# One kernel of attention and routed experts: the last attention round kept apart from weight splitting, and the last two quartets routed and sent in one row ahead of the expert tiles

## What is computed

```
x = x + attn(layernorm(x), ctx, mask; Wq, Wk, Wv, Wo)
h = layernorm(x)
logits = h @ wg.T                      # 2048 rows x 8 experts
two best experts, weights renormalised
y_e = (silu(h @ w1_e.T) * (h @ w3_e.T)) @ w2_e.T
x = x + w_a * y_a + w_b * y_b
```

## Time and profile before

| what | us |
|---|---|
| median of three runs | 288.73 |
| profiled execution, its span | 289.2 |
| PE busy in it | 220.1 (76%) |
| DVE busy | 214.5 (74%) |
| ACT busy | 131.9 (46%) |
| POOL busy | 109.8 (38%) |

### The profile page before, as it was taken

How to read it: one execution, slowest core, us unless ns; L and a number is a source line. 1 busy time by engine, 2 the same in 40 slices (tenths; PEclk the granted TensorE clock), 3 DMA queues, 4 the chain that set the end, 5 groups by cost and what they waited for, 6 DMA issues and landing times.

```text
span 289.2 us, 5289 instructions
## 1 busy us (share of the span) xinstructions
PE 220.1 (76%) x1445; PEld 161.4 (56%) x1445; DVE 214.5 (74%) x619; ACT 131.9 (46%) x291; POOL 109.8 (38%) x120
## 2 busy tenths in 40 slices
PE   0787779998989988887667674688787789997620
PEld 0663456666757665665336542477566668886410
DVE  4779966688759867895977786568895568775596
ACT  5777127554665448342145546243334435453300
POOL 4310350121403070105486556104556565555530
PEclk9996579999999999979756799589899999999855
DMA  6954411353033302331602110421342232211807
GB/s 216 318 233 118 131 35 28 92 125 86 9 98 96 94 0 67 87 100 47 207 9 67 46 39 29 99 47 30 77 79 76 82 84 73 80 52 26 236 5 217
DMA packets 38108, 26.33 MB, mean 91 GB/s; under 512 B 4748, under 2 KB 35726, under 8 KB 37696
## 3 DMA queue, kind: packets, MB, share of 16 engines
q1 hardware_dynamic: 34848, 19.76, 25.5%
q0 software_dynamic: 2656, 5.40, 6.1%
q10 hardware_dynamic: 576, 0.83, 0.9%
HBM read 12.32 MB, written 6.31 MB: 64 GB/s over the span
## 4 chain that ended last, share of the span: by engine, by line
PE 42%; DVE 30%; issue 10%; SPq 8%; DMA 4%; ACT 2%; POOL 1%; another core or an unknown queue 1%; DVEq 0%; ACTq 0%; POOLq 0%
SPq L427 8%; PE bank L528 8%; DVE m_neg L1411 6%; PE bank L759 4%; PE bank L760 3%; PE bank L733 3%; PE bank L652 3%; DMA bd<-st 3%; PE bank L746 3%; PE bank L736 3%; PE bank L693 2%; PE bank L676 2%; PE bank L734 2%; PE bank L679 2%; PE bank L534 2%
## 5 line engine op out<-in xcount | busy, mean ns | idle before, releaser
L1411 DVE TENSOR_REDUCE m_neg<-bank 128x4 f32<-128x512 f32 x64 | 43.5, 684 | 15.4 <-PE bank L693 15.0
L1048 POOL DMA_INDIRECT ys<-big x39 | 38.1, 976 | 40.0 <-DVE big L1447 19.2
L923 ACT ACTIVATE big<-bank 128x512 f32<-128x512 f32 x64 | 37.4, 597 | 20.9 <-PE bank L679 20.0
L797 ACT ACTIVATE st<-bank 128x128 fp32r<-128x128 f32 (+1 forms) x78 | 22.6, 330 | 31.6 <-PE bank L746 16.1
L1004 POOL DMA_INDIRECT xg<-rows,rows_i x24 | 24.6, 1027 | 31.8 <-DVE rows_i L1218 11.6
L693 PE MATMUL bank<-bd,st 128*128 128x512 f32 x64 | 31.1, 509 | 4.7 <-DMA bd<-st 3.8
L676 PE MATMUL bank<-m_bd,ones_b 128*128 128x512 f32 x64 | 31.3, 489 | 2.1 <-ACT big L923 1.9
L759 PE MATMUL bank<-bd,st 128*128 x78 | 24.3, 332 | 9.8 <-DVE big L1447 6.2
L1355 DVE SCALAR_TENSOR_TENSOR st<-st_hi,cst,bank 128x512 fp32r<-128x512 f32 x32 | 23.3, 747 | 11.3 <-ACT st_hi L797 9.0
L1026 POOL TENSOR_TENSOR m_bd<-mT,cst 128x512 fp32r<-128x512 f32 x16 | 17.3, 1110 | 30.1 <-DVE mT L1334 30.0
L679 PE MATMUL bank<-bd,st 128*128 128x512 f32 x64 | 27.1, 423 | 0.0
(11 more groups left out here) (174 smaller groups left out, 514.0 us busy)
## 6 DMA issues: line engine op xcount, KB each, us to landing
bd<-st SPq DMA_DIRECT2D x126, 64.0 KB, 2.0
big<-xg SPq DMA_DIRECT2D x39, 64.5 KB
raw<-in_L_ffn_w SPq DMA_DIRECT2D x2, 1024.0 KB, 9.3
raw<-ys SPq DMA_DIRECT2D x6, 256.0 KB
x_all<-in_x SPq DMA_DIRECT2D x4, 256.0 KB, 4.5
rows<-in_mask_BxS_if POOLq DMA_DIRECT2D x4, 256.0 KB, 5.2
ctx_all<-in_L_ffn_w SPq DMA_DIRECT2D x1, 1024.0 KB
ctx_all<-in_ctx SPq DMA_DIRECT2D x3, 256.0 KB, 5.2
```

The source lines that it names most:

```text
L923: nc.scalar.activation(prob[n % 2][:, NJ * g:NJ * (g + 1), :].rearrange("p h q -> p (h q)"), s2[k % 2][:, :], ACT.Exp, scale=SCALE).then_i ...
L1048: pool.indirect_dma_start(ys, bass.IndirectOffsetOnAxis(xt[n % XR][:, D:RW].bitcast(I32), 0), y_sb[n % YR], None, bounds_check=PAIRS - 1, ...
L1411: nc.vector.tensor_reduce(m_neg[:, H * (b - 1) + NJ * g:H * (b - 1) + NJ * (g + 1)], s1[k % s1_ring(u)][:, :].rearrange("p (j q) -> p j q" ...
```

## The change

In the last round of attention the twelve weight pieces are no longer taken together by both engines tick by tick. ACT copies one of pieces 0 to 7 behind every second exponential, and pieces 8 to 11 behind the round. DVE's part of the round is written out by hand: heads, projections and statistics of each batch as it comes, with steps of quartet 2's routing, tables and splits between them. Quartet 2's fills come later on PE. Quartet 3 is normalised, routed and placed directly behind the round, and the loop over tiles begins behind that on PE and DVE. POOL sends two rows of quartet 2, takes the inverse deviations of quartet 3, sends the other six and then all of quartet 3, ahead of any result. The ranks of a quartet no longer need the running sum per batch: PE adds the earlier batches of the quartet by three more products, so `rk` waits for `sel` and for the `cum` of the quartets before, and `cum` is kept per quartet. The four pieces of w2 are split by DVE at tiles 0 and 1, and `other_tiles` comes at tiles 3 to 5 instead of 7 to 9. SP pads before it loads tile 15, and waits for quartet 3's rows only before tile 17. The w2 load stands behind the last block-diagonal copies.

```diff
--- before
+++ after
-LAST_FILLS = {2: [("x2T", 2)], 4: [("lg", 2)], 7: [("rk", 2)], 8: [("cn", 0)]}
-WEIGHT_STEPS = {0: [0, 1], 2: [2, 3], 3: [4], 4: [5], 8: [6], 9: [7], 12: [8], 14: [9], 16: [10], 17: [11]}
+LAST_FILLS = {7: [("x2T", 2)], 9: [("lg", 2)], 15: [("rk", 2)], 17: [("cn", 0)]}
+WEIGHT_STEPS = {1: [0], 3: [1], 5: [2], 7: [3], 9: [4], 11: [5], 13: [6], 15: [7]}
...
-                if u == NQ:
-                    sp.wait_ge(work_full, slot["V", NQ - 1] + 1)
-                    sp.wait_ge(ck_ready, NQ)
-                    sp.dma_start(raw[2], w2).then_inc(in_w2, 16)
...
+                if u == NQ:
+                    sp.wait_ge(work_full, slot["V", NQ - 1] + 1)
+                    sp.wait_ge(ck_ready, NQ)
+                    sp.dma_start(raw[2], w2).then_inc(in_w2, 16)
...
-            def open_phase(f):
-
-                if f:
-                    fill_pads()
+            def read_rows(f):
+
                 sp.wait_ge(tab_ready, f + 1)
...
+            def all_sent(q):
+                for k in range(2):
+                    sp.wait_ge(sent[q][k], 16 * QB)
+
+            rows = read_rows(0)
+            for q in range(NQ - 1):
+                all_sent(q)
             sp.wait_ge(o_full, 3 * QB)
             for n in range(NT):
+                if n == XR:
+                    fill_pads()
+                    rows += read_rows(1)
                 if n == NTS[0]:
-                    rows += open_phase(1)
+                    all_sent(NQ - 1)
+                    sp.wait_ge(padded, 16 * (E + 1))
...
+                    for b in range(QB - 1):
+                        nc.tensor.matmul(o[:, (b + 1) * E:QB * E], cst[:, C_ALL:C_ALL + P],
+                                         sel[:, b, :].unsqueeze(1).to_broadcast([P, QB - 1 - b, E]), start=False, stop=False)
+                    if q:
+                        pe.wait_ge(cum_ready, q)
+                    else:
+                        pe.wait_ge(setup_ready, 1)
+                    nc.tensor.matmul(o[:, 0:QB * E], cst[:, C_ALL:C_ALL + P], cum[:, q, :].unsqueeze(1).to_broadcast([P, QB, E]),
                                      start=False, stop=True).then_inc(work_full, 1)
+                    pe.wait_ge(cum_ready, NQ - 1)
+                    parts = [cum[:, NQ - 1, :]] + ([sel[:, b, :] for b in range(QB)] if q else [])
+                    for k, part in enumerate(parts):
+                        last = nc.tensor.matmul(o[:, 0:E], cst[:, C_ALL:C_ALL + P], part, start=(k == 0), stop=(k == len(parts) - 1))
+                    last.then_inc(work_full, 1)
...
             heads_by_query(B - 1)
-            col += columns(7, 11)
             heads_by_dim(B - 1)
-            col += columns(11, 13)
             project_out(B - 1)
-            col += columns(13, NTS[0])
-            pe.wait_ge(wlo_ready, 3 * NB // 4)
+            fill(("x2T", NQ - 1))
+            fill(("lg", NQ - 1))
+            col += columns(0, NTS[0] // 2)
+            fill(("rk", NQ - 1))
+            fill(("cn", 1))
+            col += columns(NTS[0] // 2, NTS[0])
+            pe.wait_ge(wlo_ready, NB // 2)
...
-                if n == 0:
-                    fill(("x2T", NQ - 1))
-                if n == 1:
-                    fill(("lg", NQ - 1))
-                if n == 4:
-                    fill(("rk", NQ - 1))
-                if n == 5:
-                    fill(("cn", 1))
...
             take_heads(B - 1)
+            squash(2)
+            take_normalised(B - 1)
+            take_weights(8)
+            take_weights(9)
+            prepare(NQ - 1)
+            take_weights(10)
+            take_weights(11)
             nc.scalar.activation(unused[:, :], cst[:, C_ONE:C_ONE + 1], ACT.Silu)
-            take_normalised(B - 1)
...
-            send_quartet(2)
-            inverse_deviation(NQ + 3)
+            send_quartet(2, 0, 2)
+            inverse_deviation(NQ + 3, 0, QB - 1)
+            inverse_deviation(NQ + 3, QB - 1, QB)
+            send_quartet(2, 2)
+            send_quartet(NQ - 1)
...
-                    send_quartet(NQ - 1)
...
+            def last_statistics(b):
+
+                n, m = QB * (NQ - 1) + b, 2 * NQ - 1
+                dve.wait_ge(x2_done, n + 1)
+                row_statistics(QB * (NQ - 1), b)
+                dve.wait_ge(dve_done, marked[0])
+                ins = nc.vector.bn_aggr(mv[:, m, b, :], stats[:, b, :])
+                if b >= QB - 2:
+                    ins.then_inc(var_ready, 1)
...
-                    own(nc.vector.tensor_scalar(sel[:, :, :], rank[:, :, :], 2.0, None, ALU.is_lt))
+                    nc.vector.tensor_scalar(sel[:, :, :], rank[:, :, :], 2.0, None, ALU.is_lt).then_inc(sel_ready, 1)
                 if k == 2:
-                    for b in range(QB):
-                        ins = nc.vector.tensor_tensor(cum[:, QB * q + b + 1, :], cum[:, QB * q + b, :], sel[:, b, :], ALU.add)
-                        dve.wait_ge(dve_done, mark(ins))
-                    nc.vector.tensor_tensor(ew[:, :, :], sel[:, :, :], lg[:, :, :], ALU.mult).then_inc(sel_ready, 1)
+                    for i in range(2):
+                        mark(nc.vector.tensor_scalar(which[:, :, i, :], rank[:, :, :], float(i), None, ALU.is_equal))
                     dve.wait_ge(sel_ready, q + 1)
+                    mark(nc.vector.tensor_reduce(chosen[:, :], sel[:, :, :].rearrange("p b e -> p e b"), X, ALU.add))
+                    own(nc.vector.tensor_tensor(ew[:, :, :], sel[:, :, :], lg[:, :, :], ALU.mult))
+                    if q + 1 < NQ:
+                        nc.vector.tensor_tensor(cum[:, q + 1, :], cum[:, q, :], chosen[:, :], ALU.add).then_inc(cum_ready, 1)
...
-            normalise_heads(B - 1)
-            take_projection(B - 1)
-            second_statistics(NQ - 1)
+            first = QB * (NQ - 1)
+            take_projection(first - 1)
+            second_statistics(2)
+            place_rows(1)
+            weigh(1)
+            normalise(2 * QB, NQ + 2)
+            rest_of_weights(0)
+            rest_of_weights(1)
+            normalise_heads(first)
+            routing_step(2, 0)
+            take_projection(first)
+            routing_step(2, 1)
+            normalise_heads(first + 1)
+            last_statistics(0)
+            routing_step(2, 2)
+            take_projection(first + 1)
+            place_rows(2)
+            normalise_heads(first + 2)
+            last_statistics(1)
+            full_tiles(0)
+            take_projection(first + 2)
+            rest_of_weights(2)
+            normalise_heads(first + 3)
+            last_statistics(2)
+            rest_of_weights(3)
+            take_projection(first + 3)
+            last_statistics(3)
+            full_tiles(1)
+            full_tiles(2)
+            weigh(2)
+            normalise(first, 2 * NQ - 1)
+            rest_of_weights(4)
+            rest_of_weights(5)
+            for k in range(3):
+                routing_step(NQ - 1, k)
+            place_rows(NQ - 1)
+            rest_of_weights(6)
+            rest_of_weights(7)
+            full_tiles(3)
             rest_of_tile(0)
             for n in range(NT + 3):
                 if n + 1 < NT:
                     rest_of_tile(n + 1)
-                if n == 0:
-                    normalise(QB * (NQ - 1), 2 * NQ - 1)
+                if n in (0, 1):
+                    rest_of_weights(8 + 2 * n)
+                    rest_of_weights(9 + 2 * n)
...
-                if 1 <= n < 4:
-                    routing_step(NQ - 1, n - 1)
-                if n == 4:
-                    place_rows(NQ - 1)
-                if 7 <= n < 10:
-                    other_tiles(n - 7)
+                if 3 <= n < 6:
+                    other_tiles(n - 3)
```

More of the change, by code:

```diff
@@ L200, in program @@
         wgT = sb("wgT", [P, E])
-        cum = sb("cum", [P, B + 1, E])
+        cum = sb("cum", [P, NQ, E])
+        chosen = sb("chosen", [P, E])
         which = sb("which", [P, QB, 2, E])
@@ L461, in open_phase @@
                                                                  min_val=0, max_val=E * REG, skip_runtime_bounds_check_because=IN_RANGE)
-                for q in (range(3) if f == 0 else range(3, NQ)):
-                    for k in range(2):
-                        sp.wait_ge(sent[q][k], 16 * QB)
-                if f:
-                    sp.wait_ge(padded, 16 * (E + 1))
-                return list(at)
-            rows = open_phase(0)
+                return list(at)
+            def all_sent(q):
[4 more added lines that the diff above has]
+                all_sent(q)
             sp.wait_ge(o_full, 3 * QB)
             for n in range(NT):
+                if n == XR:
+                    fill_pads()
+                    rows += read_rows(1)
                 if n == NTS[0]:
-                    rows += open_phase(1)
+                    all_sent(NQ - 1)
+                    sp.wait_ge(padded, 16 * (E + 1))
                 if n >= XR:
@@ L582, in fill @@
                     o = claim(name)
```

(44 more changed lines are left out.)

12 lines of the change are left out of this document (4 added, 8 removed).

## The result

The changed kernel takes 279.7 us (median of 4 runs, 277.0 to 282.2) beside 288.35 for the kernel before on the same chip: the ratio is 0.966, with a 95% interval of 0.961 to 0.971 (the ratio leaves out the execution of 282.2 us, which lay over 1.5% above the quickest, so it is not 279.7 / 288.35). It is faster by 3.4%, where I had forecast 292.9 and slower. The profiled execution of after has a span of 278.3 us beside 289.2.

A forecast was written before the change was run, and what follows sets the result against it. Hand-overs, with no engine full, were taken to bound attention's last round, and TensorE most late tiles. 289.2 - 6.7 (attention) + 14.9 (row) - 4.0 (loop) = 293.4 profiled, so 292.9 us as the time; range 287.5 to 297.5.

The forecast's parts named there:

- The step that failed: POOL ahead of the tiles: quartet 3's eight sends before the first result's scatter were costed at nothing.
- T0: Start of the tile loop's first product on TensorE, forecast 14.9 us later relative to Y than before.
- the tail after tile 38: End of the kernel behind tile 38: claimed untouched by the change, at 20.5 us.
- Rival B: 27 intervals after tile 11: results no longer pile up around quartet 3's sends, pace 1.76 or less, 285.9 us; chance 0.12.
- Attention: Last attention round: both TensorE stalls go, exponentials close up; gain 6.7 us, between 4 and 9.5.
- rival A: Last attention round: ScalarE alone paces it, gain the full 9.5 us, time 290.1, no change; chance 0.20.
- rival C: Last attention round: weight copies and in-order VectorE replace the stalls, gain only 2 us, time 297.6; chance 0.15.
- The row: Quartet 3's serial routing between attention and the tiles: T0 = Y + 17.3 instead of Y + 2.45, costing 14.9 us.
- Y: Start of the last projection's addition at the end of attention, forecast near 175.8 us.
- The loop to tile 11: First tile intervals: without quartet 3's routing VectorE loses small instructions; gain 4.0 us, between 1.5 and 6.5.
- The 27 late intervals: Tiles 11 to 38, 54.6 us at 2.02 each: pace taken as TensorE's own, to stay near 2.0.
- the sign that I had set for being wrong: Late tiles after tile 11 running at 1.76 or less; others were attention gaining 9 us or more, or a much shorter row.

The follow-up runs named there:

- routing_in_loop: sends_behind with the last quartet's fills, steps and table put back among the tiles, attention's new order left; 288.82 us, ratio 1.000 to the kernel before.
- before_once_more: The kernel before, unchanged, profiled for one more execution; span 283.9 us.
- sends_behind: The changed kernel with the last quartet's eight sends put back behind the second result on POOL; 289.67 us, ratio 1.001 to the kernel before.
- before_deep: The kernel before with each result waiting for the landing of the one four ahead, not two; 279.39 us, ratio 0.969.
- loop_deep: routing_in_loop with each result waiting for the landing of the one four ahead, not two; 279.31 us, ratio 0.970 to the kernel before.
- row_only: The kernel before with only quartet 3's routing, sends and table moved as in the changed kernel, attention left alone; 287.87 us, ratio 0.998.

## Why the prediction was wrong, point by point

*The step that failed* is in the part on the row: "tiles 17 and on wait for them, but tile 17 comes more than 30 us after T0, so I cost this at nothing". I asked of the eight sends only which loads wait for them, not what stands behind them on POOL. Behind them stand 37 results, and the row has no time to spare: two in flight, it goes at 1.7 to 1.8 us an issue (77 to 82 us for 46 steps), no faster than the tiles make results (1.64). From the same step comes "the tail after tile 38 (20.5 us) is untouched": it was 20.5, 23.2, 26.5 and 28.3 us in before, after, routing_in_loop and before_once_more, since it hangs on POOL and not on tile 38. By POOL's row the change is one subtraction: 196.62 - 185.85 = 10.8 earlier, 0.4 longer, 0.5 less behind it, 10.9 in all, the difference of the spans. For this pair of executions that is bookkeeping, since in mine of before the tiles ended with the row; that the row sets the time is shown by sends_behind, before_deep and loop_deep.

*Rival B* (0.12) named the right queue and the wrong harm. It looked for the pile in the tiles' pace, and I turned it down because TensorE was busy 29.0 of 31.15 us. That stretch holds 17 of the 27 intervals, at 1.83 each; the longest ones, up to 3.7 us, lie outside it, so it could not speak for a pace of 2.02. The tiles did run at 1.64 per tile in after, under its 1.76, but so they did in before_once_more (1.63).

*Attention*, 6.7 with bounds of 4 and 9.5: 9.2, close to the 9.5 of rival A and far from the 2 of rival C. The exponentials took 17.8 us instead of 26.75, beside 17.2 that I had worked out as ScalarE's floor. The mechanism was right; the middle of the bounds was not. But as a term of the sum it was wrong too: in routing_in_loop it moves tile 0 not at all, for the line through quartet 2's sends, which I had put beside the new row, already stood beside attention's end in the old order, and the change put quartet 3's deviations into it.

*The row*, T0 = Y + 17.3: it was Y + 18.76. To x2T 5.2 (5.6 forecast), from there to the row ids 9.9 (8.3), from there to T0 3.6 (3.45). The stretch was granted 0.50 and x2T took 1.12, as forecast; the ranks, 2.3 from 181.79, were put too low, at 1.5, and so were the logits, 1.85 from 176.87, at 1.3. "Slower" followed from a term that was right in size and that row_only shows to cost nothing.

*The loop to tile 11*, 4.0 with bounds of 1.5 and 6.5: 6.7, a little over the upper bound, which was all of VectorE's small instructions.

*The 27 late intervals*, nothing: -10.4 in the two profiles read, nothing that can be told between the kernels (before 44.1 to 54.6, after 44.2 in one execution). The nothing was right by luck: it rested on the 54.6 of the earlier trace rows, which was no property of the kernel. So the sign that I had set for being wrong, 1.76 or less, came up without meaning rival B; the one for attention, 9 us or more, came up too.

## What to carry to other kernels

List the queues that issue in order to the very end, and cost each one like an engine: first issue, number of issues, pitch with its waits for landing, what follows the last. Busy time hides such a row (POOL showed 17.0 of 31.15 us in the middle of that row), and one execution's chain can hide it behind another line that happened to run late, so look at a second execution before trusting which line is last. When a queue is bound by landings, put its independent issues where it would idle, or let more be in flight: here one number gave as much as the whole change.

## What the runs showed of the hardware

An indirect transfer occupies POOL 0.97 us and the next follows 1.28 us after it at best. With two in flight the pitch was 1.55 in the pairs shown and 1.7 to 1.8 over the row: a result landed 2.1 to 4.8 us after its issue began (in most cases near 2.3), and the result that waited for it began 0.85 us later at the earliest. With four in flight the pitch was 1.28, in before_deep for 24 results in a row (216.15 to 245.49). When the reads of the results run beside them at the end, results 33 and 34 took 4.8 to 6.2 us to land in all the runs that have it on record (5.77 in the chain of before_once_more). The Trainium skill, "DMA: Bandwidth & Descriptors", on the anatomy of a DMA issued from GpSimd, says that about 2 us of such a transfer are fixed and that most of it is the wait for the write's receipt, not the making of descriptors. Landings mostly near 2.3 and the gain from more in flight agree with it; what part of a landing is the receipt no run here shows; the 1.28 us that each issue holds POOL is a floor that these runs show beside it.

TensorE's clock was no surprise: it was granted 0.50, the 1.2 GHz level, through the serial row, in which TensorE worked 8.2 of 18.7 us; 0.92 on average in the 22.4 us behind it; and 1.00, the 2.4 GHz level, from tile 11 to tile 38.
